# Turning the normalised x by a DMA transpose, and two moves on POOL, in a gated cross-attention and FFN kernel

## The reference

```python
x = x + tanh(g_xattn) * attention(layernorm(x), ctx, ctx, Wq, bq, Wk, bk, Wv, bv, Wo, bo)   # 16 heads of 16
x = x + tanh(g_ffn) * ffn(layernorm(x), w_gate, w_up, w_down)    # absmax-quantised activations, 4-bit block weights

q = Q @ Wq.T + bq ; k = K @ Wk.T + bk ; v = V @ Wv.T + bv
attn = softmax(q k^T / sqrt(16)) ; out = (attn v) @ Wo.T + bo
layernorm(x) = (x - mean) / sqrt(var + 1e-5)
```

## Time and profile before

| what | value |
|---|---|
| median of 3 runs | 610.08 us (609.75 to 610.86) |
| the profiled execution's own time | 608.44 us |
| its span, first to last instruction | 606.6 us |
| granted TensorE clock, mean | 0.986 of full speed |
| PE busy | 567.0 us, 93% |
| DVE busy | 489.4 us, 81% |
| ACT busy | 439.2 us, 72% |
| POOL busy | 217.8 us, 36% |

### The profile page before, as it was taken

How to read it: one execution, slowest core, us unless ns; L and a number is a source line. 1 busy time by engine, 2 the same in 40 slices (tenths; PEclk the granted TensorE clock), 3 DMA queues, 4 the chain that set the end, 5 groups by cost and what they waited for, 6 DMA issues and landing times. The chain is left out here.

```text
span 606.6 us, 11827 instructions
## 1 busy us (share of the span) xinstructions
PE 567.0 (93%) x4353; PEld 343.8 (57%) x4353; DVE 489.4 (81%) x836; ACT 439.2 (72%) x632; POOL 217.8 (36%) x239
## 2 busy tenths in 40 slices
PE   2679999999999999999987899999999899989998
PEld 1446666666566666666446444444444344458887
DVE  5687889999999988998828699979888799954442
ACT  2227888778788877887765445449999998869960
POOL 4621358766567879755355070000000000010100
PEclk9789999999999999999989999999999999999999
DMA  6532444454544454333232000000000000013442
GB/s 193 136 88 73 140 125 126 131 148 134 144 140 142 128 137 125 100 109 104 69 97 71 2 0 1 1 0 2 0 1 0 1 0 1 2 69 105 140 139 105
DMA packets 42813, 48.98 MB, mean 81 GB/s; under 512 B 10436, under 2 KB 30532, under 8 KB 42756
## 3 DMA queue, kind: packets, MB, share of 16 engines
q1 hardware_dynamic: 40916, 43.38, 24.4%
q0 software_dynamic: 1408, 4.46, 2.5%
q10 hardware_dynamic: 432, 0.39, 0.3%
HBM read 24.32 MB, written 8.70 MB: 54 GB/s over the span
## 5 line engine op out<-in xcount | busy, mean ns | idle before, releaser
L886 DVE TENSOR_REDUCE negm<-s_ps 128x2 bf16<-128x512 f32 x256 | 163.0, 680 | 23.3 <-PE s_ps L520 21.9
L702 ACT ACTIVATE pt<-st_ps 128x512 f32<-128x512 f32 x256 | 138.8, 596 | 49.0 <-PE st_ps L535 48.0
L1227 PE MATMUL pairs<-xq,wut 128*128 128x512 f16 x576 | 124.7, 379 | 2.8 <-ACT lnall L1387 1.7
L1227 PEld LDWEIGHTS pairs<-xq,wut 128*128 128x128 f16 x576 | 56.2, 98 | 71.2 <-issue 2.4
L520 PE MATMUL s_ps<-kst,qst 96*128 96x256 f16 x512 | 81.5, 278 | 9.2 <-DVE negm L886 4.4
L535 PE MATMUL st_ps<-qst,kst 97*128 97x512 f16 x256 | 77.2, 382 | 1.8 <-DMA qst<-mrow 1.0
L459 PE MATMUL pv_ps<-pt,vt 128*32 128x256 f32 x1024 | 68.5, 385 | 0.7 <-ACT pt L702 0.6
L1695 POOL PARTITION_ALL_REDUCE vmax<-vmax x5 | 1.8, 368 | 173.0 <-DVE vmax L1494 119.9
L520 PEld LDWEIGHTS s_ps<-kst,qst 96*128 96x128 f16 x512 | 44.6, 98 | 32.4 <-DVE negm L886 17.5
L1227 PE MATMUL pairs<-xq,wgt 128*128 128x512 f16 x276 | 60.5, 379 | 0.0
L1006 POOL TENSOR_SCALAR xn<-xt,mv,rstd 128x256 f32<-128x256 f32 x30 | 36.7, 1230 | 57.1 <-PE misc L595 56.9
(11 more groups left out here) (224 smaller groups left out, 1047.1 us busy)
## 6 DMA issues: line engine op xcount, KB each, us to landing
qst<-qk SPq DMA_DIRECT2D x96, 64.0 KB, 2.0
kst<-qk SPq DMA_DIRECT2D x45, 128.0 KB, 3.3
xt<-in_x SPq DMA_DIRECT2D x16, 256.0 KB, 4.3
ct<-in_ctx SPq DMA_DIRECT2D x16, 256.0 KB, 2.9
xr<-in_x SPq DMA_DIRECT2D x16, 256.0 KB, 4.0
out<-y SPq DMA_DIRECT2D x16, 256.0 KB, 3.6
lnall<-out POOLq DMA_DIRECT2D x8, 512.0 KB, 4.3
recb<-rec_dram SPq DMA_DIRECT2D x15, 256.0 KB
```

The costliest lines, as they stand in the source:

```text
L702: nc.scalar.activation(pt[:, (j // 2) % 2, j % 2, kt], st_ps[u % 3][:], ACT.Exp, scale=1.0 / (WS * WS * HD ** 0.5)).then_inc(exp_done, 1)
L886: nc.vector.tensor_reduce(negm[:, b % 2, tt, lo:lo + 5:4], s_ps[tt][:], AX.X, ALU.max, negate=True).then_inc(max_done, 1)
L1227: mm = nc.tensor.matmul(ps[:, p, k, :], w[:, a, dt, f * P:(f + 1) * P], xq[:, b, c, dt, :], start=n == 0, stop=n == len(terms) - 1)
```

## The change

1. **x is turned by a DMA.** For every batch but the first, PE's four transposes go. In step 6 ACT copies the token-major `xn` (SBUF) to the float16 high half `xtok[:, 0]`, and DVE subtracts for the low half `xtok[:, 1]`, both one step earlier than before. In step 7 ACT waits for that (`xl_done`), and issues one `dma_start_transpose` of 128 x 1024 float16 (256 KB) from `xtok` to `xtr`. PE's q projection waits for its landing (`x_turned`). POOL's `normalise` now waits for `xl_done` where it waited for `xt_done`.
2. **The low half `al` moves** from DVE to POOL for batches 0 to 13, still in step 5.
3. **POOL's LayerNorms are written as a product and a sum**: x * rstd + (-mean * rstd), with both factors per partition. `shift_of` makes the second one by two instructions of 128x2 and two waits.
4. `ln_max` on DVE moves from step 6 to step 7, and the FFN's `unread_work` goes with its semaphores.

```diff
             def normalise(b):
...
                     pool.wait_ge(rstd_done, b + 1)
-                    pool.wait_ge(xt_done, b)
+                    shift_of(mv[:, :, 0], rstd[:], nrstd[:], shift[:], shifted, b - 1)
+                    pool.wait_ge(xl_done, b)
                     for tt in range(KT):
-                        op = nc.gpsimd.tensor_scalar(xn[:, tt, :], xt[:, b % 3, tt, :], mv[:, tt, 0:1],
-                                                     rstd[:, tt:tt + 1], ALU.subtract, ALU.mult)
+                        op = nc.gpsimd.tensor_scalar(xn[:, tt, :], xt[:, b % 3, tt, :], rstd[:, tt:tt + 1],
+                                                     shift[:, tt:tt + 1], ALU.mult, ALU.add)
...
+            def shift_of(mean, r, negative, to, done, b):
+
+                nc.gpsimd.tensor_scalar(negative, r, -1.0, 0.0, ALU.mult, ALU.add).then_inc(done, 1)
+                pool.wait_ge(done, 2 * b + 1)
+                nc.gpsimd.tensor_tensor(to, mean, negative, ALU.mult).then_inc(done, 1)
+                pool.wait_ge(done, 2 * b + 2)
...
+                if (b := batch(g, 21)) is not None and b < LAST - 1:
+                    pool.wait_ge(ah_done, b + 1)
+                    pool.wait_ge(o_done, b)
+                    nc.gpsimd.tensor_tensor(al[:], at[:, b % 2], ah[:], ALU.subtract).then_inc(al_done, 1)
...
@@ vector
-                if (b := batch(g, 21)) is not None and b < LAST - 1:
-                    low_of(b)
-                if (b := batch(g, 30)) is not None and b < LAST - 1:
+                if (b := batch(g, 31)) is not None and b < LAST - 1:
                     ln_max(b)
...
-                if (b := batch(g, -17)) is not None:
+                if (b := batch(g, TURN)) is not None and b:
                     dve.wait_ge(xh_done, b + 1)
-                    nc.vector.tensor_tensor(xl[:], bank(PAIRS * b + TURN)[:], xh[:], ALU.subtract).then_inc(xl_done, 1)
+                    nc.vector.tensor_tensor(xtok[:, 1], xn[:].rearrange("p t d -> p (t d)"), xtok[:, 0], ALU.subtract
+                                            ).then_inc(xl_done, 1)
...
@@ scalar
-                if (b := batch(g, -17)) is not None:
-                    act.wait_ge(xt_done, b + 1)
+                if (b := batch(g, TURN)) is not None and b:
+                    act.wait_ge(xn_ready, b + 1)
+                    act.wait_ge(x_turned, 16 * (b - 1))
+                    nc.scalar.copy(xtok[:, 0], xn[:].rearrange("p t d -> p (t d)")).then_inc(xh_done, 1)
+                if (b := batch(g, TURN + 1)) is not None and b:
+                    act.wait_ge(xl_done, b + 1)
                     act.wait_ge(q_done, b)
-                    nc.scalar.copy(xh[:], bank(PAIRS * b + TURN)[:]).then_inc(xh_done, 1)
+                    act.dma_start_transpose(xtr[:].rearrange("p i t u q -> p (i t u) q"),
+                                            xtok[:].rearrange("p i c -> p (i c)")).then_inc(x_turned, 16)
...
@@ tensor
-                    pe.wait_ge(xl_done, b + 1)
+                    if b:
+                        pe.wait_ge(x_turned, 16 * b)
+                    else:
+                        pe.wait_ge(xl_done, 1)
...
-                if (b := batch(g, TURN)) is not None:
-                    pe.wait_ge(top_done[0], before(g, TOP0))
-                    pe.wait_ge(ql_done, before(g, Q))
-                    pe.wait_ge(xl_done, b)
-                    pe.wait_ge(xn_ready, b + 1)
+                if g == TURN:
+                    pe.wait_ge(xn_ready, 1)
```

More of the change, by code:

```diff
@@ L96, in attention @@
         rstd = sb("rstd", [P, KT], F32)
-        xh = sb("xh", [P, 2, S], F16)
-        xl = sb("xl", [P, 2, S], F16)
+        nrstd = sb("nrstd", [P, KT], F32)
+        shift = sb("shift", [P, KT], F32)
+        xtok = sb("xtok", [P, 2, KT * D], F16)
+        xtr = sb("xtr", [P, 2, KT, 2, P], F16)
         ch = sb("ch", [P, 2, S], F16)
@@ L151, in attention, with two_halves @@
         recx = wi[:, 0:4 * S].bitcast(F32)
-        ahl, all_ = (xh, ch), (xl, cl)
+        def two_halves(i):
+            return xtr[:, i].rearrange("p t u q -> p (t u q)").rearrange("p (u s) -> p u s", u=2)
+        ahl, all_ = (two_halves(0), ch[:]), (two_halves(1), cl[:])
         ident_zeroed = sem("ident_zeroed")
@@ L246, in attention @@
         rstd2_done = sem("rstd2_done")
+        shifted = sem("shifted")
+        shifted2 = sem("shifted2")
         ln_done = sem("ln_done")
@@ L554, in _ @@
                     pe.wait_ge(ql_done, b)
-                    pe.wait_ge(xl_done, b + 1)
+                    if b:
+                        pe.wait_ge(x_turned, 16 * b)
+                    else:
+                        pe.wait_ge(xl_done, 1)
                     pe.wait_ge(weights_low, 3)
-                    project(bank(g), "q", xh, xl, q_done)
+                    project(bank(g), "q", lambda k: xtr[:, 0, :, k, :], lambda k: xtr[:, 1, :, k, :], q_done)
                 if (b := batch(g, K)) is not None:
                     pe.wait_ge(top_done[1], before(g, TOP1))
-                    pe.wait_ge(xl_done, before(g, TURN))
+                    pe.wait_ge(top_done[0], before(g, TOP0))
+                    pe.wait_ge(ql_done, before(g - 1, Q))
                     pe.wait_ge(kl_done, b)
                     pe.wait_ge(cl_done, b + 1)
-                    project(bank(g), "k", ch, cl, k_done)
+                    project(bank(g), "k", lambda k: ch[:, k, :], lambda k: cl[:, k, :], k_done)
                 if g == -12:
@@ L663, in high_last @@
                 act.wait_ge(v_done, NB)
-                nc.scalar.copy(ahl[v][:], at[:, 1 - v]).then_inc(ah_last, 1)
+                nc.scalar.copy(ahl[v], at[:, 1 - v]).then_inc(ah_last, 1)
             def high_of(b):
@@ L690, in _ @@
                     high(1, bank(PAIRS * b + K), kh_done)
-                if (b := batch(g, -17)) is not None:
-                    act.wait_ge(xt_done, b + 1)
+                if g == TURN + 1:
+                    act.wait_ge(xt_done, 1)
+                    nc.scalar.copy(xtr[:, 0].rearrange("p t u q -> p u t q"),
+                                   bank(TURN)[:].rearrange("p u (t q) -> p u t q", t=KT)).then_inc(xh_done, 1)
+                if (b := batch(g, TURN)) is not None and b:
[4 more added lines that the diff above has]
+                    act.wait_ge(xl_done, b + 1)
                     act.wait_ge(q_done, b)
-                    nc.scalar.copy(xh[:], bank(PAIRS * b + TURN)[:]).then_inc(xh_done, 1)
+                    act.dma_start_transpose(xtr[:].rearrange("p i t u q -> p (i t u) q"),
+                                            xtok[:].rearrange("p i c -> p (i c)")).then_inc(x_turned, 16)
                 if 0 <= it < NB:
@@ L937, in _ @@
                     ln_max(LAST)
-                if (b := batch(g, -17)) is not None:
+                if g == TURN + 1:
+                    dve.wait_ge(xh_done, 1)
+                    nc.vector.tensor_tensor(xtr[:, 1].rearrange("p t u q -> p u t q"),
+                                            bank(TURN)[:].rearrange("p u (t q) -> p u t q", t=KT),
+                                            xtr[:, 0].rearrange("p t u q -> p u t q"), ALU.subtract).then_inc(xl_done, 1)
+                if (b := batch(g, TURN)) is not None and b:
                     dve.wait_ge(xh_done, b + 1)
-                    nc.vector.tensor_tensor(xl[:], bank(PAIRS * b + TURN)[:], xh[:], ALU.subtract).then_inc(xl_done, 1)
+                    nc.vector.tensor_tensor(xtok[:, 1], xn[:].rearrange("p t d -> p (t d)"), xtok[:, 0], ALU.subtract
+                                            ).then_inc(xl_done, 1)
                 if g == -11:
@@ L1043, in _ @@
                         pool.wait_ge(rstd2_done, b + 1)
+                        shift_of(mv2[:, b % 2, :, 0], rstd2[:, b % 2], nrstd2[:], shift2[:], shifted2, b)
                         for tt in range(KT):
-                            nc.gpsimd.tensor_scalar(t["lnall"][:, b, tt * D:(tt + 1) * D], y[:, b % 2, tt, :], mv2[:, b % 2, tt, 0:1],
-                                                    rstd2[:, b % 2, tt:tt + 1], ALU.subtract, ALU.mult).then_inc(ln_done, 1)
+                            nc.gpsimd.tensor_scalar(t["lnall"][:, b, tt * D:(tt + 1) * D], y[:, b % 2, tt, :],
+                                                    rstd2[:, b % 2, tt:tt + 1], shift2[:, tt:tt + 1], ALU.mult, ALU.add
+                                                    ).then_inc(ln_done, 1)
                 if (b := batch(g, -28)) is not None and b:
@@ L1672, in _ @@
         def _(pool):
[L1673 to L1691, removed]
             def over_partitions(n, i):
```

27 lines of the change are left out of this document (10 added, 17 removed).

## The result

| | before | changed |
|---|---|---|
| median | 610.47 us (4 runs beside it) | 641.45 us (637.67 to 646.46, 4 runs) |
| ratio, 95% interval | | 1.0516 [1.0474, 1.0557] |
| the profiled execution | 608.44 us | 646.46 us |

The changed kernel is 31 us slower. The profiled execution of the changed kernel is the slowest of its four, 38 us above the profile of before.

What follows compares the result with a forecast made beforehand. PE was taken to bound the steady attention, with DVE close behind. Terms -7.0 (transposes) + 18.6 (new wait) + 3.0 (transpose DMA) + 8.0 (clock) = +22.6 us on 610.08, giving 632.7 us, range 612 to 655.

Steps and rivals of the forecast that it cites:

- the clock: Granted clock falling after PE's new waits: 1.6 us a fall, half of ten taken, 8.0 us; bounds 0 and 16.0.
- The term for the transposing DMA: PE's q projection waiting for the DMA's landing, taken as 4.3 us: 1.0 each in batches 1, 3 and 4, together 3.0.
- The transposes on PE: Four transposes leave PE between v products and next scores: 0.50 us a batch, batches 2 to 15, 7.0 us gained.
- The new wait: PE's output projection in step 7 waits for POOL's `al` behind two `xn`: 1.8 us, ten times, 18.6 with a DMA issue.
- Where it happens: Wait for `al` only where a normalisation stands ahead of it: steps 20 to 93, batches 0 to 9, none for 10 to 13.
- Rival 2: Transposing DMA turns eight blocks in series, 15.2 us, so PE waits at q, 146 us together: 768 us; chance 0.10.
- Its issue on ACT: Issuing the transposing DMA holds ACT about 0.67 us, covered in ten periods because ACT idles while PE waits.
- three rows that I had: Earlier clock readings: PE busy 1.42 of 3 us with clock 0.51, then 0.50 later; 1.02 us of idling left it at 1.00.
- POOL's form elsewhere and the unread work: Outside the wait's chain, cheaper LayerNorm scalars on POOL and removal of the FFN's unread work: costed at nothing.
- DVE's `al` is worth nothing: DVE loses `al`, 14 times 0.6 us, but is no bound while PE waits, so nothing is gained.
- `ln_max` one step later: Moving `ln_max` on DVE to step 7 is covered, since DVE idles there behind `xl`.
- Rival 1: The wait isn't there because POOL gives `al` within 2.8 us of the scores: faster, 606.1 us; chance 0.08.

Runs made afterwards that it cites:

- al_first: Changed kernel with one offset moved, so POOL normalises in step 5 behind the low half, not in step 4 ahead of it: 608.04 us, run again 607.48 us.
- form_alone: Kernel before with POOL's LayerNorms as product and sum and without the unread work, nothing else: 608.4 us, 0.9978 of before.
- tail_alone: Kernel before without the unread work and its semaphores, nothing else: 609.21 us, 0.9998 of before.
- clock_held: Changed kernel with seven matmuls of overwritten result ahead of PE's wait for the low half, in nine of the ten waits: 624.32 us, 1.0245 of before.
- change_again: The changed kernel run once more, unaltered, for a second profile: 644.63 us, 1.057 of before.
- al_pool_alone: Kernel before with only the low half moved to POOL, keeping PE's transposes and the old LayerNorm form: 654.19 us, 1.0718 of before.
- al_dve: Changed kernel with the low half of the attended rows back on DVE in step 5, the rest kept: 609.95 us, 0.9991 of before.
- mixed: The kernel of al_first, but PE turns batches 0 to 4 and the DMA turns batches 5 to 15: 606.33 us, 0.9937 of before.

## Why the prediction was right

The forecast was 632.7 us, in a range of 612 to 655; the measurement is 641.45. The mechanism held at each step that decides, and one term, the clock, was half of what it should have been. The term for the transposing DMA was 2.2 us too high and hid a part of that, which is luck.

- **The transposes on PE**: 0.50 us a batch, 7.0 in all. Measured 0.48 a period (17.31 to 16.83), which is right for the steady part. Ahead of batch 0's projection, where four of the fourteen batches stand, no saving shows: it starts at 93.67 and 94.12 in `al_first`, and at 93.61, 92.28 and 94.95 in `before`, `form_alone` and `tail_alone`.
- **The new wait**: 1.8 us, ten times, 18.6 with the one longer by a DMA issue. Measured 20.3: nine of 1.95 to 2.05 and one of 2.56. The chain took 5.02 us instead of 4.65: `xn` 0.56 instead of 0.5, and hand-overs between engines that I had at 0.15 to 0.2 in all. They were 0.18 (DVE to POOL) and 0.25 (POOL to PE) in the first wait. PE's own work over the chain took 3.01 us there, where I had 2.83, and 5.02 less 3.01 is the wait. The ends of the range for `xn`, 0.38 and 0.77, hold it. The estimate of 0.38 by the rate per element of the Trainium skill (page "GPSIMD Engine Reference", section "Elementwise — side-by-side cycle accounting") was too low here, though its 512-element figure agreed with a row; from 561 ns at 256 elements to 767 at 512 the time grows by much less than double.
- **Where it happens**: batches 0 to 9, none for 10 to 13. Right.
- **The transpose DMA**: landing taken as 4.3, measured 4.0 (3.2 to 5.1). In the ten periods nothing waits for it. In the batches without a projection I had three waits of 1.0; the profile shows 0.8, once, and the second one 1.4, once. The term of 3.0 was too large. Rival 2 is out. So is the estimate of eight blocks in series at the 1309 ns of the Trainium skill, page "VectorE: DVE Perf Modes", section "The three transpose paths"; its sentence there on about 90% of DMA bandwidth fits what was measured, a landing like that of a plain DMA of this size (4.1 for `xt` in the same profile).
- **Its issue on ACT**: I took 0.67 from a plain DMA; it holds ACT for 1.38. Covered in the waits, as said; in `al_first` it may be part of the late exponentials, which wasn't tried apart.
- **The clock**: here the size was off. I took a fall after half of the ten waits, 8.0 us. A fall followed all ten in the profile, and nine of ten in the second one; at 1.65 each, ten are 16.5, and `clock_held` gives back 14 to 17. This is the term that was mis-sized: of its two bounds, 0 and 16.0, the upper one was right. Of the three rows that I had the earlier trace rows, a wait of 1.8 us is nearer to the first than to the third, but that reading wouldn't have been safe: the runs also have waits of 1.95 us (`clock_held`, `change_again`) and of 3.1 us (`al_pool_alone`) with no fall behind them.
- **POOL's form elsewhere and the unread work**, costed at nothing: `form_alone` and `tail_alone` bear it out, with intervals that reach from 0.5% faster to 0.2% slower. That DVE's `al` is worth nothing is borne out less closely: `al_dve` and `al_first` lie 1.9 us apart, within their spread. `ln_max` one step later wasn't tried alone.

With the measured terms: -6.7 + 20.3 + 0.8 + 16.5 = +30.9, against 31.0 between the medians. That it fits so well is partly luck, since the terms are read from an execution that lies 38.0 us above the profiled one of before. In the second profile they give -6.7 + 20.3 + 1.4 + 14.9 = +29.9, against 34.0.

The terms are tested best in the nine periods, where PE has no other new wait: -4.3 for nine times the transposes, 18.3 for nine waits, 14.9 for nine falls, together 28.9, against 28.5 measured. The rest lies outside. Ahead of batch 0's projection there are 5.6 us, of which 2.0 are the first wait and 0.8 the one for `xtr`. The new wait of batch 0's k projection, 2.1 us, was in none of my terms, and the clock stood lower from 30 to 40 us (0.59, before 0.84); how the rest divides between these two isn't settled. Behind the start of batch 9's projection there are 4.0 us, of which 1.65 is one fall. The two executions of `al_first` differ there by as much (2.6 and 1.4 us), so nothing shows that the remainder is the change's own.

Rival 1 was refuted as an outcome, but its number, 606.1 if the wait were not there, can be held against `al_first` and `al_dve`: 607.5 to 610. Two things explain part of the difference. The start gains nothing, as said above. And beyond nine times their plain period, the nine periods have 1.9 to 4.7 us of small waits in `al_first`, `al_dve` and `mixed`, where the three kernels with a period of 17.31 and no wait for POOL's `al` have 0.7 to 2.7; these executions are too few to give the difference a size.

## What to carry to other kernels

When work moves to an idle engine, look at what stands ahead of it in that engine's queue. POOL had 4.6 us to spare in each period, but spent them at the head of its queue in a wait, so work behind it got none of it; one step's difference in order was worth 33 us. A wait on PE of 2 us in a stretch that is otherwise full can cost nearly the same again through the clock (1.65 us here), and filling matmuls show how much. Work taken from the engine that is the bound may come back only in part: here it was 1.5 to 2.1 of 7 us, with waits for loads, for ACT and for a new semaphore in its place.

## What the runs showed of the hardware that was not expected

- On POOL, `tensor_scalar` with two per-partition factors takes 561 ns for 128x256 float32 as product and sum, and 1230 as difference and product.
- One transposing DMA of 128x1024 float16 holds ACT's queue for 1.25 to 1.70 us, twice a plain one (0.65), and lands in 4.0. The DMA queue of ACT has 15840 packets more than before, 1056 for each transpose, all of them under 512 B, and yet it lands like a plain transfer of 256 KB.
- A longer wait doesn't always cost a fall: in `al_pool_alone` waits of 3.1 us left the clock at 1.00 for four periods (from 96 to 179 us), and four of the next five periods had a fall; in the changed kernel a wait of 2.0 us was followed by a fall in 19 of 20 cases, and in `clock_held` the one wait of that length that stayed empty was not. What tells these apart stays open.
